# Audio tower on one core: feature transform with its 192 distinct columns, ranks of the routing in bf16

## What is computed

```python
def _L0_tok_ref(x, ...):                  # B, S, D = 64, 125, 192
    h = depthwise conv over tokens (7 taps); pointwise matmul D x D; relu
    h = max over pairs of tokens          # 62 tokens are left
    y = jnp.real(jnp.fft.fft2(h))         # over the 62 tokens and the 192 features
    return layernorm(y) * gamma + beta
h = h + attention(layernorm(h))           # 8 heads, relative positions
h = h + quantised_ffn(layernorm(h))       # ternary weights, 8-bit activations, 512 wide
h = h + local_attention(layernorm(h))     # 12 heads of 16
# last layer: each token goes to the one of 8 experts with the largest router probability
out = silu(x @ w1[e]) * (x @ w2[e]) @ w3[e], times that probability
```

## Time and profile before

| | |
|---|---|
| median of 3 runs | 1221.06 us (1220.58 to 1223.4) |
| the profiled execution | 1219.23 us, span 1217.4 us |
| PE busy | 1026.1 us (84%) |
| ACT busy | 839.4 us (69%) |
| DVE busy | 796.2 us (65%) |
| POOL busy | 368.0 us (30%) |
| mean granted PE clock | 0.937 |

### The profile page before, as it was taken

The page is one execution under the profiler, slowest core; times in us unless marked ns, Lnnn a source line. Parts: engine busy times, 40 slices in busy tenths (PEclk is TensorE's granted clock), DMA queues, the critical chain, the costliest instruction groups (busy, mean ns, idle before and its releaser), DMA issues. The chain is left out here.

```text
span 1217.4 us, 31083 instructions
## 1 busy us (share of the span) xinstructions
PE 1026.1 (84%) x9342; PEld 770.1 (63%) x9375; DVE 796.2 (65%) x2640; ACT 839.4 (69%) x2673; POOL 368.0 (30%) x1099
## 2 busy tenths in 40 slices
PE   3667999899999999998999999999998651999996
PEld 1445666666666666666666666666666430888885
DVE  2355777777777777777777777777776532455553
ACT  1436888888888888888888888888887530333331
POOL 1112333333333333333333333333333212122222
PEclk9787999999999999999999999999999655999998
DMA  6135111111111111111111111111111006222221
GB/s 222 32 103 166 35 39 39 38 38 44 38 38 38 54 41 46 41 38 38 38 38 44 38 38 38 43 49 42 46 34 32 8 7 212 55 60 61 57 58 41
DMA packets 73487, 65.85 MB, mean 54 GB/s; under 512 B 39341, under 2 KB 63696, under 8 KB 73328
## 3 DMA queue, kind: packets, MB, share of 16 engines
q1 hardware_dynamic: 63232, 46.66, 13.0%
q0 software_dynamic: 4512, 12.52, 3.1%
q10 hardware_dynamic: 5712, 6.29, 1.8%
HBM read 36.80 MB, written 28.95 MB: 54 GB/s over the span
## 5 line engine op out<-in xcount | busy, mean ns | idle before, releaser
L1186 DVE SCALAR_TENSOR_TENSOR conv_lo<-xT_lo,c_taps,conv_lo 128x248 f32<-128x248 f32 x192 | 89.8, 468 | 22.6 <-ACT xT_hi L895 22.6
L1131 ACT ACTIVATE e_tanh<-bank_a 128x512 f32<-128x512 f32 x34 | 20.3, 597 | 103.9 <-PE bank_a L587 103.9
L1081 ACT ACTIVATE p<-bank_b,max 128x62 f32<-128x62 f32 x384 | 81.4, 351 | 0.0
L496 POOL TENSOR_TENSOR var_y<-ssq_y,c_eps 128x1 f32<-128x1 f32 x32 | 6.1, 192 | 241.3 <-ACT f_sq L1051 241.3
L587 PE MATMUL bank_a<-e_xT,w_now 128*128 128x128 f32 x544 | 70.5, 284 | 5.7 <-DVE e_gate L1460 1.4
L587 PEld LDWEIGHTS bank_a<-e_xT,w_now 128*128 128x128 f32 x544 | 64.9, 196 | 14.9 <-issue 12.0
L587 PE MATMUL bank_a<-c_wv,a_xT 64*64 64x384 f32 (+1 forms) x512 | 74.0, 503 | 0.0
L587 PE MATMUL bank_a<-a_xT,c_wq 64*128 64x128 f32 (+1 forms) x512 | 71.7, 282 | 0.0
L587 PE MATMUL bank_a<-c_wo,oT 128*128 128x192 f32 x384 | 68.8, 330 | 0.6 <-ACT oT L895 0.6
L587 PE MATMUL bank_a<-a_xT,c_wk 64*128 64x128 f32 (+1 forms) x512 | 69.0, 281 | 0.0
L987 ACT ACTIVATE p<-bank_a,max 128x62 f32<-128x62 f32 x256 | 55.6, 329 | 19.2 <-DVE max L1246 19.2
(11 more groups left out here) (262 smaller groups left out, 3038.8 us busy)
## 6 DMA issues: line engine op xcount, KB each, us to landing
rel_scores<-rel_tok SPq DMA_DIRECT2D x32, 492.0 KB, 2.6
rel_skew<-rel_scores SPq DMA_DIRECT2D x64, 124.0 KB, 3.1
x_tok<-in_x SPq DMA_DIRECT2D x32, 187.5 KB
e_rest<-routed SPq DMA_DIRECT2D x34, 97.0 KB, 1.9
e_tok<-routed SPq DMA_DIRECT2D x34, 96.0 KB, 2.0
routed<-pad_rows SPq DMA_DIRECT2D x8, 386.0 KB, 3.2
w_sb<-in_w ACTq DMA_DIRECT2D x1, 3072.0 KB, 12.5
w_sb<-in_w ACTq DMA_DIRECT2D x2, 1024.0 KB, 14.4
```

The lines of the kernel that those rows point to most:

```text
L496: pool.tensor_tensor(out=var[k][:, :], in0=ssq[k][:, :], in1=c_eps[:, width:width + 1], op=ALU.mult).then_inc(var_eps[k], 1)
L1081: last = nc.scalar.activation(p1[:, h, 0:T], src[:, at * T:(at + 1) * T], ACT.Exp, bias=max1[:, mx:mx + 1])
L1131: nc.scalar.activation(e_tanh[:, :], pa0[:, :], ACT.Tanh, scale=0.5).then_inc(e_tanhr, 1)
L1186: c.mark(v.scalar_tensor_tensor(conv_lo[:, :, :], xT_lo[:, :, k:k + PAIRS], c_taps[:, 0, k:k + 1], conv_lo[:, :, :], ALU.mult, ALU.add))
```

## The change

The cosine columns of a real transform are even around the middle and the sine columns odd: column 192 - k of the cosines is column k, and of the sines it is minus column k. So `c_dft` keeps only cosine columns 0 to 96 (NC = 97) and sine columns 1 to 95, 192 in all, and `z_sb` and its copy are 192 wide. The second transform writes output columns 0 to 96 from the cosine and sine columns, and output columns 97 to 191 from the same columns read backwards (`z_sb[:, NC - 2:0:-1]`), with a third table, +S, for the sines. It now has four matmuls instead of two. Apart from that, `chosen` and the two tables that it is multiplied by become bf16, which holds zeros and ones exactly; the bf16 ones are set by a memset on POOL, the bf16 triangle by a copy on DVE in the first `b_rotate`.

```diff
+NC = D // 2 + 1
-        c_dft = lp("c_dft", [P, 3, 2 * D])
-        c_dft_seq = lp("c_dft_seq", [P, 2, P])
+        c_dft = lp("c_dft", [P, 3, D])
+        c_dft_seq = lp("c_dft_seq", [P, 3, P])
-        z_sb = lp("z_sb", [P, 2 * D])
+        z_sb = lp("z_sb", [P, D])
-        chosen = lp("chosen", [P, NE + 1])
+        chosen = lp("chosen", [P, NE + 1], BF16)
+        c_tri16, ones16 = lp("c_tri16", [P, P], BF16), lp("ones16", [P, P], BF16)
@@ gpsimd
+            pool.memset(ones16[:, :], 1.0)
             pool.memset(ones[:, :], 1.0).then_inc(cleared, 1)
@@ tensor
             def t_dft(m):
                 pe.wait_ge(t_h, m + 1)
-                mm(pt[:, 0:2 * D], hT[:, 0:2, :].rearrange("p b s -> p (b s)"), c_dft[:, 0, :], stop=False)
+                mm(pt[:, 0:D], hT[:, 0:2, :].rearrange("p b s -> p (b s)"), c_dft[:, 0, :], stop=False)
                 for b in range(2):
-                    mm(pt[b * TP:(b + 1) * TP, 0:2 * D], hT[:, 2, :], c_dft[:, 1 + b, :], start=False).then_inc(t_z, 1)
+                    mm(pt[b * TP:(b + 1) * TP, 0:D], hT[:, 2, :], c_dft[:, 1 + b, :], start=False).then_inc(t_z, 1)
             def t_dft_seq(m):
                 pe.wait_ge(t_zs, m + 1)
-                mm(pt[:, 0:D], c_dft_seq[:, 0, :], z_sb[:, 0:D], stop=False)
-                mm(pt[:, 0:D], c_dft_seq[:, 1, :], z_sb[:, D:2 * D], start=False).then_inc(t_y, 1)
+                cosines, sines = z_sb[:, 0:NC], z_sb[:, NC:D]
+                mm(pt[:, 0:NC], c_dft_seq[:, 0, :], cosines, stop=False)
+                mm(pt[:, 1:NC - 1], c_dft_seq[:, 1, :], sines, start=False)
+                mm(pt[:, NC:D], c_dft_seq[:, 0, :], z_sb[:, NC - 2:0:-1], stop=False)
+                mm(pt[:, NC:D], c_dft_seq[:, 2, :], z_sb[:, D - 1:NC - 1:-1], start=False).then_inc(t_y, 1)
             def r_rank(m):
-                mm(pa0[:, RK:RK + NE + 1], c_tri[:, :], chosen[:, :])
-                mm(pa0[:, TT:TT + NE + 1], ones[:, :], chosen[:, :]).then_inc(r_ranked, 1)
+                mm(pa0[:, RK:RK + NE + 1], c_tri16[:, :], chosen[:, :])
+                mm(pa0[:, TT:TT + NE + 1], ones16[:, :], chosen[:, :]).then_inc(r_ranked, 1)
@@ scalar
-                copy(z_sb[:, :], pt[:, 0:2 * D]).then_inc(t_zs, 1)
+                copy(z_sb[:, :], pt[:, 0:D]).then_inc(t_zs, 1)
@@ vector, b_rotate, first tile only
+                    setup(v.tensor_copy(c_tri16[:, :], c_tri[:, :]))
@@ tables
-    full = np.concatenate([np.cos(ang), np.sin(ang)], 1)
+    full = np.concatenate([np.cos(ang[:, 0:NC]), np.sin(ang[:, 1:NC - 1])], 1)
-        seq[s, 0, s], seq[s, 1, s] = np.cos(ang), -np.sin(ang)
+        seq[s, 0, s], seq[s, 1, s], seq[s, 2, s] = np.cos(ang), -np.sin(ang), np.sin(ang)
```

More of the change, by code:

```diff
@@ L1488, in _tables @@
     ang = 2 * np.pi * np.outer(np.arange(D), np.arange(D)) / D
-    full = np.concatenate([np.cos(ang), np.sin(ang)], 1)
-    dft = np.zeros((P, 3, 2 * D), np.float32)
+    full = np.concatenate([np.cos(ang[:, 0:NC]), np.sin(ang[:, 1:NC - 1])], 1)
+    dft = np.zeros((P, 3, D), np.float32)
     dft[:, 0], dft[:KB, 1], dft[KB:, 2] = full[:P], full[P:], full[P:]
@@ L1493, in _tables @@
     ang = 2 * np.pi * np.outer(np.arange(T), np.arange(T)) / T
-    seq = np.zeros((P, 2, P), np.float32)
+    seq = np.zeros((P, 3, P), np.float32)
     for b in range(2):
         s = slice(b * TP, b * TP + T)
-        seq[s, 0, s], seq[s, 1, s] = np.cos(ang), -np.sin(ang)
+        seq[s, 0, s], seq[s, 1, s], seq[s, 2, s] = np.cos(ang), -np.sin(ang), np.sin(ang)
     c["dft_seq"] = seq
```

## The result

The changed kernel takes 1208.12 us (median of 6 runs, 1203.77 to 1209.22) against 1220.57 for the kernel before on the same chip (6 runs, 1218.9 to 1223.4): ratio 0.9889, 95% interval 0.9873 to 0.9904. The forecast was 1208. The profiled execution took 1207.81 us, span 1205.9, against 1219.23 and 1217.4.

A forecast was written before the change was run, and what follows sets the result against it. No engine is full; waits among PE, ACT and DVE bound the tile, the feature transform on the path. Tile -8.1, start -1.5, clock -3.4 sum to -13.0, forecasting 1208 us; own range 1203 to 1213, with rivals 1199 to 1217.

The forecast's parts named there:

- The feature transform: PE, each tile: half the columns, four steps losing 0.16 us each, 0.64 us; rel_skew starts that much earlier.
- The second transform: PE, each tile: eight records at 0.11 us make 0.88 where four made 0.65, 0.23 us more.
- The reversed read: PE's second transform: backward operands cost what forward ones cost; rival (3), 0.33 us a record, gives 1235, chance 0.06.
- What becomes late next: Through the tile: PE newly waits on z; 0.51 us becomes 0.29 at f_gate; 28 tiles give -8.1 us.
- DVE's max: DVE, behind rel_skew: could start 0.64 us earlier, but `chosen` holds DVE, so it gains 0.51.
- PE's wait for p: PE, behind the ranks, waiting for ACT's exponentials: 0.89 us before, near 0.85 after.
- The copy of z: ACT: 192 columns instead of 384, 0.32 us instead of 0.49, 0.17 less; its start not PE's doing.
- The ranks: PE, ahead of its wait for p: bf16 saves 0.3 us of work, which the wait absorbs, so 0.
- The loads: Before the first matmul: 224 KB less at 237 GB/s, 0 to 1.0 us, taken as 0.5.
- The first tile: At half clock: transform loses 1.28 us, copy loses 0.17, second transform gains 0.1 to 0.9, taken as 0.5.
- The clock: In the loop: four of five falls gone at 0.85 us each, -3.4 us, with 0 to -4.2 as ends.
- thin stretch: PE, from the end of the b-transposes, the ranks alone in it: 1.40 us becomes 0.97, speaking for fewer falls.

The follow-up runs named there:

- exponentials split: Changed kernel with ACT's twelve exponentials of the second attention cut into nine, the copy of z, then three: 1202.04 us, ratio 0.9831.
- two-matmul kernel: Changed kernel with the second transform as two matmuls of 192 columns instead of four of 95 to 97: 1206.46 us, ratio 0.9866.
- forward kernel: Changed kernel with the second transform's two reversed operands read in ascending order: 1207.76 us, ratio 0.9872.
- wide copy: Changed kernel with ACT's copy of z 384 columns long again, writing z twice: 1215.66 us, ratio 0.9935.
- large-table run: Changed kernel with c_dft loaded at its old size, the upper half zeros and unused: 1212.81 us, ratio 0.9914.
- ranks thrice: Kernel before with its two rank matmuls issued three times over, writing the same values: 1217.54 us, one time.
- changed twice: The changed kernel itself, unaltered, in its first runs and again beside later ones: 1208.12 us, then 1209.49 us.
- f32 ranks: Changed kernel with the bf16 ranks taken back to f32, the transforms as changed: 1207.92 us, ratio 0.9864.
- second square: Changed kernel with ACT squaring f_y twice, the first into a buffer nothing reads: 1215.34 us, one time.

## Why the prediction was right, point by point

The forecast rests on the tile and on the clock, and both came out as reckoned and for the reasons given, the clock's as far as the runs go. That the total hit 1208 to a tenth is luck: six executions of the changed kernel spread over 5 us, and terms outside the loop were off by 1 to 3 us in both directions.

**The feature transform** gave 0.64 us and rel_skew starts 0.64 earlier, as reckoned from the earlier trace rows.

**The second transform** was priced by its weight loads: eight records, 0.11 each. That holds. Without a wait ahead of it (exponentials split) it takes 0.86 us from start to start, 0.108 a record; with the wait 0.97. The difference is in the first step alone: from the first record to the second it is 0.19 us with the wait (648.42 to 648.61) and 0.08 without (642.32 to 642.40), so one weight load stands in the open, as the working had it. The two-matmul kernel shows the price from the other side. The reversed read is free, which the forward kernel shows. The rule taken from the Trainium skill (Advanced Engine Details and Errata, Memory Cachelines) said the same, and the run agrees with it; that it is the reason no run here shows.

**What becomes late next.** All three waits came where the working had put them: z, stats_t (0.47 us against 0.35 expected), f_gate (0.20 against 0.2). DVE's max gained 0.61, not 0.51: it was held to end behind `chosen`, but starts at 648.45 while chosen is drawn until 648.54. The step took durations of neighbouring DVE rows as if they could not overlap; they do by 0.09. It did not matter for the tile, as f_gate waits for the other branch. PE's wait for p is 0.70, where the working had near 0.85. The copy of z came out right at its end, 0.19 earlier against 0.17, but not in its parts: its row is only 0.07 shorter (0.42 against 0.49) and starts 0.12 earlier. The working said that its start was not PE's doing. It was: the copy starts 0.31 us behind ACT's last exponential in the kernel before and 0.20 in the changed one, which is the distance of the exponentials among themselves. So before, the copy had waited 0.11 us for the wide transform. A copy that follows the exponentials with no wait is drawn longer (384 columns 0.58 in the wide copy, 0.49 before), which made up for it. The tile gained 0.314 against 0.29: **-8.8** against -8.1.

**The ranks** were costed at 0 and are 0, both ways, because PE's wait for p is behind them.

**The loads** were mis-sized: **-2.2** against -0.5, outside the 0 to -1.0. The step took the bytes at the mean rate of all queues. The large-table run puts the difference on that table, more than its bytes explain: each small table behind it lands later, c_feat last of all.

**The first tile** was expected to give 1.0 us, and between the two profiled executions it gave nothing (+0.4 to the fourth tile). The early part came out as priced: from the first matmul to the second transform 14.21 us instead of 15.65, 1.44 less, where the working had 1.28 and 0.17. Behind that, the profiled execution of the kernel before was an exception. PE works at half its speed there by the durations, and only in that execution did it reach full speed as early as the second transform. These are its next eight records, then the same place in the kernel before with the bf16 ranks, then in the changed kernel:

```profile
27.77 1.15 PE L587 MATMUL bank_a<-c_feat,c_wrk 32*128 32x123 f32 x8
```

```profile
26.17 1.65 PE L589 MATMUL bank_t<-z_sb,c_dft_seq 128*128 128x192 f32 x4 [0.62 <-ACT z_sb L897]
27.75 2.06 PE L589 MATMUL bank_a<-c_feat,c_wrk 32*128 32x123 f32 x8
```

```profile
23.27 2.02 PE L590 MATMUL bank_t<-z_sb,c_dft_seq 128*128 128x97 f32 x8 [0.46 <-ACT z_sb L901]
25.23 2.06 PE L590 MATMUL bank_a<-c_feat,c_wrk 32*128 32x123 f32 x8
```

The kernel before, profiled again, and the one with the ranks thrice show 2.07 and 2.06 there as well. Like with like, at half speed, the second transform takes 1.95 us from start to start instead of 1.58, 0.37 longer, where the working allowed 0.1 to 0.9. The records on c_feat start 16.16 us behind the first matmul instead of 17.23: the first tile gives 1.07 us. To the fourth tile the four executions of kernels with the old transforms take 110.7 us in the mean (109.6 to 111.9), and five with the transforms of the change (changed twice, f32 ranks, forwards, large table) 109.6 (108.8 to 110.0). So the term was right, and the pair of profiles hid it. The granted clock shows 1.00 in these stretches, so the level is read from the durations alone; why one execution reached full speed earlier stays open.

**The clock** gave all five falls, **-3.8** against -3.4. The reason given was the thin stretch between the transposes, 1.40 us then and 0.97 expected; it is 0.90 now. The table of the falls bears it out as far as it goes: the kernels with 1.39 to 1.40 us fall, those with 1.20 or less do not, and with the stretch filled the falls go at its full length. Idle time alone does not sort them (0.89 us with falls, 1.01 without). What is not settled is how much of the credit in the changed kernel goes to this stretch: the transforms and the period of the tile changed with it, and only the run with the ranks thrice holds them fixed. The period by itself is no likely reason, as the second square has 27.98 us and no fall. That the wider matmuls of the old transforms play a part is not excluded.

The rule of the Trainium skill (TensorE: Matmul & The Clock Gate, Part 4, PE-mode transpose), that transposes do not count, had pointed to the longer stretch from the second transform to the first matmul with vBD. It is 2.81 us in the kernel before, 2.31 in the changed one, 2.62 with the split, and sorts the kernels as well as the other does. The ranks issued thrice leave it at 2.80 (632.85 - 630.05) and have no falls, so its length alone is not what decides either. The ranks are no transposes, so this does not speak against the rule; nor does any run here show that transposes count less.

**The experts**, which the change does not touch, took 2.6 us more, and the working had no term for it. In the profiled execution of the kernel after, three of the 33 steps last 5.47 us instead of 4.90, as here on DVE from 1037.64 to 1043.11:

```profile
1032.74 0.43 DVE L1462 COPY w_now<-w_sb 128x512 f32 x1 [2.82 <-PE bank_a L590]
...
1037.64 0.43 DVE L1462 COPY w_now<-w_sb 128x512 f32 x1 [1.90 <-PE bank_a L590]
...
1043.11 0.43 DVE L1462 COPY w_now<-w_sb 128x512 f32 x1 [2.35 <-PE bank_a L590]
```

The count of such steps goes from 0 to 13 over the thirteen profiled executions, and the stretch from 183.0 to 190.8 us. The kernel before had none in one execution and three in the next, the changed one three and eleven. So this pair of profiles shows no effect of the change. It does not follow that there is none: the four executions with the old transforms have 0, 3, 5 and 7 such steps, the nine with the new ones 3 to 13, 8 in the mean, and at 0.57 us each that would be some 2.4 us of loss that the working has no term for. The ranges overlap, and it stays open. Nor are the steps spread evenly: the last step is among them in all executions but the first. Their cause stays open. It also means that the kernel before was profiled in a lucky execution; with three such steps its span would have been 1.7 us longer. Another 0.7 of the 2.6 lies ahead of the first expert's tanh.

Between the two profiles the errors partly cancel: loads -1.7, first tile and fill +1.4, loop -1.1, drain and experts +3.0 make about +1.5 on the span (11.5 gained, 13.0 forecast).

## What to carry to other kernels

When an f32 matmul is cut up, see whether its columns or its records set the time. Going from 384 to 192 columns gave all the time of the columns. Going from 192 to 97 gave only a third of a record's time, 0.16 to 0.11 us, which is what 9 columns cost too, and the number of records doubled. Follow a saved stretch to the place where two chains meet: here half was lost at f_gate to the chain through z, and moving three exponentials behind a copy won it back. A thin place of PE can cost clock elsewhere in the tile, and filling it with work of no use took 4.3 us off this loop, in one execution. Profile the kernel before more than once: a single one here hid 1 us of the first tile's gain, and showed 2.6 us of loss in the experts that its next execution more than halves.

## What the runs showed of the hardware

- A moving operand read with step -1 costs what a forward read costs (tile 27.74 us either way, eight records 1.13).
- In a row of matmul records with 128 f32 weight columns each, the records stood 0.11 us apart with 9, 95, 97 or 128 moving columns. Only the step from the first record to the second was shorter: 0.03 us with 9 columns (630.70 to 630.73, ranks thrice), 0.08 with 97 (642.32 to 642.40, exponentials split).
- Where PE waited for its moving data, eight such records took 0.11 us more (0.97 against 0.86), one weight load.
- The granted clock can show 1.00 while matmuls run at half speed: at the start of the kernels, where eight records on c_feat took 2.06 to 2.07 us in twelve executions and 1.15 in one.
- A row without a bracket can still be held: with the new transforms f_gate started 0.03 to 0.04 us behind qscale_y, with a bracket and without, because the row ahead of it on ACT was drawn past its start.
- Four to seven falls of the clock in 28 tiles, 0.85 us each, went away when PE's 0.89 us of waiting in each tile was filled with useless records of nine columns (one execution).
